# Value products of an attention as half-row pairs of two heads, with the other TensorE work gathered in fewer places

## The reference

```python
xn, ln = layernorm(ctx), layernorm(latents)          # 77 and 1024 rows of 256
q = (ln @ Wq) -> 16 heads of 64;  k, v = concat([xn, ln]) @ Wkv -> 16 heads of 64
qn, kn = rmsnorm(q) * 64**-0.5, rmsnorm(k)
attn = softmax(where(mask, qn @ kn.T, -max))         # 1024 queries x 1101 keys
x = x + (attn @ v) @ Wout + bout
x = x + moe(layernorm(x))                            # shared expert + top 2 of 8, gelu
```

## Time and profile before

| what | us |
|---|---|
| median of 3 runs | 2591.28 (2587.12 to 2591.97) |
| the profiled execution | 2582.26 |
| its span, first to last instruction | 2580.4 |
| TensorE busy (matmuls) | 2469.2, 96% |
| TensorE weight loads | 1899.8, 74% |
| VectorE, ScalarE, GpSimdE busy | 1737.1, 1677.3, 1275.5 |
| TensorE's mean granted clock | 0.984 of 2.4 GHz |

### The profile page before, as it was taken

One profiled execution on the slowest core, in us unless ns is written; L12 is line 12 of the kernel. 1 busy time (PEld: TensorE's weight loads), 2 busy tenths in 40 slices (PEclk: granted clock), 3 DMA queues, 4 the chain that ended last, 5 costly groups with the idle time before them and its releaser, 6 DMA issues. The chain is left out here.

```text
span 2580.4 us, 46535 instructions
## 1 busy us (share of the span) xinstructions
PE 2469.2 (96%) x15720; PEld 1899.8 (74%) x15720; DVE 1737.1 (67%) x2516; ACT 1677.3 (65%) x2286; POOL 1275.5 (49%) x783
## 2 busy tenths in 40 slices
PE   3799999999999999999999999997989999999997
PEld 3566666666666666666666666656989999999997
DVE  7666766666667666676666666765876557767675
ACT  2577877787778777787788777883333344454443
POOL 4445434453455445543455344522534526666665
PEclk8899999999999999999999999998989999999999
DMA  5423422233223322332223322246822459999996
GB/s 182 155 81 92 129 87 76 84 121 104 82 78 125 103 78 86 99 121 86 78 88 122 97 82 78 86 124 128 175 84 77 141 185 318 326 317 319 323 323 170
DMA packets 231441, 361.76 MB, mean 140 GB/s; under 512 B 59559, under 2 KB 139739, under 8 KB 227400
## 3 DMA queue, kind: packets, MB, share of 16 engines
q1 hardware_dynamic: 204694, 301.66, 38.0%
q0 software_dynamic: 25696, 58.82, 8.2%
q10 hardware_dynamic: 978, 0.34, 0.1%
HBM read 280.90 MB, written 79.85 MB: 140 GB/s over the span
## 5 line engine op out<-in xcount | busy, mean ns | idle before, releaser
L826 ACT ACTIVATE pr_hi<-ps_s 128x1024 fp32r<-128x1024 f32 x512 | 524.6, 1025 | 262.0 <-PE ps_s L948 260.7
L717 DVE TENSOR_TENSOR pr_lo<-ps_s,pr_hi 128x1024 fp32r<-128x1024 f32 x288 | 351.8, 1221 | 257.1 <-ACT ps_s L827 256.9
L962 PE MATMUL ps_o<-pr_hi,vA 128*65 128x512 f32 x1152 | 472.4, 410 | 1.4 <-DVE o_first L646 0.8
L717 DVE TENSOR_TENSOR pr_lo<-pr,pr_hi 128x1024 fp32r<-128x1024 f32 x288 | 354.3, 1230 | 163.7 <-ACT pr L827 163.7
L964 PE MATMUL ps_o<-pr_lo,vA 128*65 128x512 f32 x1152 | 454.0, 394 | 0.0
L963 PE MATMUL ps_o<-pr_hi,vC 128*65 128x512 f32 x1152 | 452.9, 393 | 0.0
L455 POOL TENSOR_TENSOR sq<-raw 128x1024 f32<-128x1024 f32 (+1 forms) x96 | 134.1, 1397 | 625.3 <-ACT raw L771 625.3
L1613 ACT ACTIVATE ht<-f_ps_h,b 128x256 f32<-128x256 f32 x440 | 184.5, 471 | 339.6 <-PE f_ps_h L1545 306.4
L1545 PE MATMUL f_ps_h<-xT_hi,w 128*128 128x256 f32 x1760 | 355.1, 285 | 2.4 <-DVE xT_lo L1647 2.3
L917 PE MATMUL ps_m<-w_sb,lnT_sb 128*128 128x384 f32 (+1 forms) x1728 | 349.2, 341 | 4.2 <-DVE q_lo L659 2.5
L917 PEld LDWEIGHTS ps_m<-w_sb,lnT_sb 128*128 128x128 f32 x1728 | 298.2, 191 | 59.7 <-issue 36.4
(11 more groups left out here) (214 smaller groups left out, 4394.9 us busy)
## 6 DMA issues: line engine op xcount, KB each, us to landing
w<-w1S_dram SPq DMA_DIRECT2D x160, 512.0 KB, 6.3
lnT_sb<-lnT_dram SPq DMA_DIRECT2D x31, 2304.0 KB, 9.0
w2raw<-in_L_ffn_Wproj SPq DMA_DIRECT2D x78, 512.0 KB, 6.4
w1S_dram<-cut POOLq DMA_DIRECT2D x36, 512.0 KB, 3.0
rec<-rden_dram SPq DMA_DIRECT2D x63, 256.0 KB, 3.7
routed_dram<-empty POOLq DMA_DIRECT2D x28, 387.0 KB, 3.6
xt<-routed_dram SPq DMA_DIRECT2D x39, 258.0 KB
w_raw<-in_L_xattn_Wkv SPq DMA_DIRECT2D x66, 128.0 KB, 3.7
```

The lines of the kernel that those rows point to most:

```text
L717: v.tensor_tensor(pr_lo[:, ring(w, d), :], full_of(d), pr_hi[:, ring(w, d), :].bitcast(F32), ALU.subtract).then_inc(s_lo, 1)
L826: act.activation(pr_hi[:, ring(w, d), :], ps_s[:, d % 2, :], ACT.Exp, bias=bias)
L962: mm(out, upper, pr_hi[:, r, cols], start=k == 0, stop=False)
```

## The change

- Value products become products of 64 rows (`values_half`). A key tile's upper 64 keys and its lower 64 keys are given to the two heads at the same time, one head in rows 0 to 63 and the other in rows 64 to 127, each into its own bank; a unit later (part 1) the same tile is done with the two halves swapped. In each step of the loop the second half of unit d - 3 and the first half of unit d - 2 have the same assignment of rows to banks. A unit has six pairs, three in each part. The second part waits for its own first part (`s_half`). Only the very last units keep 128-row products.
- TensorE goes unit by unit: scores, jobs, second half, first half; at units 2 and 11 (`BETWEEN`), where a group ends, the jobs stand between the halves.
- Jobs are gathered: turns two by two at units 2 and 4 and one at 6, projections at 6 (one) and two by two at 8, 11, 13, 15. They stay 128-row products; `project_halves` is there for units in `HALVED`, which is empty.
- The full exponentials go to `pr` in units 0, 1, 9, 16 and 17 (`SPARED`), else back to `ps_s`; the waits follow.
- VectorE copies both heads' outputs in one instruction, once both are done; `invert`, `divide`, `squares` and `values` move to other units.

```diff
+TURNED = {2: (0, 1), 4: (2, 3), 6: (4,)}
+PROJECTED = {6: (0,), 8: (1, 2), 11: (3, 4), 13: (5, 6), 15: (7, 8)}
+HALVED = ()
+BETWEEN = (2, 11)
+SPARED = (0, 1, 9, 16, 17)
...
-            return pr[:, 0, :] if d % 2 else ps_s[:, 0, :]
+            return pr[:, d % 2, :] if d in SPARED else ps_s[:, d % 2, :]
...
-                wait(dve, s_pv0, w.n(2, h + 1 - 2 * before))
-                v.tensor_copy(o_sb[h][0:DH + 1, 0:512], ps_o[0:DH + 1, 0, :]).then_inc(s_o, 1)
                 wait(dve, s_pv, w.n(UNITS, KT * (h + 1) - UNITS * before))
-                v.tensor_copy(o_sb[h][0:DH + 1, 512:N], ps_o[0:DH + 1, 1, :]).then_inc(s_o, 1)
+                v.tensor_copy(o_sb[h][0:DH + 1, :].rearrange("p (r n) -> p r n", r=2), ps_o[0:DH + 1, :, :]).then_inc(s_o, 1)
...
-                            if d == 3:
+                            if d == 5:
                                 invert(w, 1, 1)
-                            if d == 7:
+                            if d == 9:
                                 divide(w, 1, 1)
-                        if w.attend and d == 12:
+                        if w.attend and d == 13:
                             invert(w, 0, 0)
...
-                        if w.turn and d in (2, 4):
-                            values(w, d == 4)
-                        if w.proj and d in (11, 15):
-                            squares(w, (d - 11) // 4)
+                        if w.turn:
+                            for i in TURNED.get(d, ()):
+                                turned(w, i)
+                        if w.turn and d in (3, 5):
+                            values(w, d == 5)
+                        if w.proj and d in (14, 17):
+                            squares(w, (d - 14) // 3)
...
-                        if d == 0 and not (isinstance(w.v, int) and (w.v == -1 or 2 * w.v + w.s == WINDOWS - 1)):
+                        if d == 2 and not (isinstance(w.v, int) and (w.v == -1 or 2 * w.v + w.s == WINDOWS - 1)):
                             squares(w, 2 - GROUPS)
...
-                        if d % 2:
+                        if d in SPARED:
                             wait(act, s_lo, w.n(UNITS, d - 1))
...
+            def weights(w, d):
...
+                return g, k, [(v_[:, slot, k, :, 0:DH + 1], p_[:, r, :]) for v_, p_ in ((vA, pr_hi), (vC, pr_hi), (vA, pr_lo))]
+
+            def begin(w, d, g, k):
+
+                pe.wait_ge(s_lo, w.n(UNITS, d + 1))
+                if k == 0:
+                    wait(pe, s_o, w.n(2, g))
...
+            def values_half(w, d, part, swap):
+
+                g, k, pairs = weights(w, d)
+                if part == 0:
+                    begin(w, d, g, k)
+                else:
+                    pe.wait_ge(s_half, w.n(UNITS, d + 1))
+                for i, (v_, p_) in enumerate(pairs):
+                    for t in range(2):
+                        h, rows = t ^ swap, slice(DH * t, DH * t + DH)
+                        ins = mm(ps_o[0:DH + 1, h, :], v_[rows, h], p_[rows, 512 * h:512 * h + 512],
+                                 start=k == 0 and part == 0 and i == 0, stop=k == KT - 1 and part == 1 and i == 2)
+                ins.then_inc(s_pv if part else s_half, 1)
...
+                    def second(d):
+                        if w.attend and not (w.first and d < LAG + 1):
+                            values_half(w, d - LAG - 1, 1, d % 2)
+
+                    def first(d):
                         if w.attend and not (w.first and d < LAG):
                             if d == LAG:
                                 pe.wait_ge(s_v, w.n(2, 2))
-                            values(w, d - LAG)
-
-                    for d in range(0, UNITS, 2):
+                            if last and d == UNITS - 1:
+                                values(w, d - LAG)
+                            else:
+                                values_half(w, d - LAG, 0, d % 2)
+
+                    for d in range(UNITS):
...
-                            wait(pe, s_lo, w.n(UNITS, d - 1))
+                            wait(pe, s_exp if (d - 2) % UNITS in SPARED else s_lo, w.n(UNITS, d - 1))
                             scores(w, d, general)
-                            if general and (d + 1) % KT == 0:
-                                maximum(w, (d + 1) // KT)
-                            wait(pe, s_exp, w.n(UNITS, d))
-                            scores(w, d + 1, general)
...
+                        elif d in BETWEEN:
+                            second(d)
+                            jobs(d)
+                            first(d)
                         else:
-                            job(d)
-                            weigh(d)
-                            job(d + 1)
-                            weigh(d + 1)
+                            jobs(d)
+                            second(d)
+                            first(d)
```

More of the change, by code:

```diff
@@ L77 @@
 TURNS = len(PARTS)
-FIRST_TURN = 2
-FIRST_PROJ = FIRST_TURN + TURNS
+TURNED = {2: (0, 1), 4: (2, 3), 6: (4,)}
[3 more added lines that the diff above has]
+SPARED = (0, 1, 9, 16, 17)
 JOBS = TURNS + KT
@@ L300, in spread @@
                 half = w.n(2, g - 2 * before)
-                wait_then(s_o, w.n(4, 2 * g + 2 - 4 * before))
+                wait_then(s_o, w.n(2, g + 1 - 2 * before))
                 sp.dma_start(rden[bass.ds(half, 1)].unsqueeze(0), o_sb[g][DH:DH + 1, :].unsqueeze(1)).then_inc(s_put, 16)
@@ L829, in window @@
                         upper(d)
[L830 to L833, removed]
+                    if w.turn:
+                        for i in TURNED.get(d, ()):
+                            turned(w, i)
+                    if w.proj:
+                        for tile in PROJECTED.get(d, ()):
+                            projected(w, tile)
                     if isinstance(w.v, int) and w.v == -1:
@@ L900, in turn, with ready @@
                 ins.then_inc(s_job, 1)
-            def project(w, tile):
-                out = ps_m[:, tile % 2, :]
+            def ready(w, tile):
                 if tile < 2:
@@ L914, in project @@
                     pe.wait_ge(s_wlo, w.n(1, 3))
-                lo = 0 if tile < NT else PW
-                for k, (a, b, c) in enumerate((a, b, c) for a, b in ((0, 0), (0, 1), (1, 0)) for c in range(C)):
+            products = [(a, b, c) for a, b in ((0, 0), (0, 1), (1, 0)) for c in range(C)]
+            def project(w, tile):
+                ready(w, tile)
+                out, lo = ps_m[:, tile % 2, :], 0 if tile < NT else PW
+                for k, (a, b, c) in enumerate(products):
                     ins = mm(out[:, lo:3 * PW], lnT_sb[:, a, c, tile * P:(tile + 1) * P], w_sb[:, w.slot, b, c, lo:],
@@ L919, in project, with project_halves @@
                 ins.then_inc(s_job, 1)
+            def project_halves(w, n, tiles, part):
+                for k, (a, b, c) in enumerate(products):
+                    for j, tile in enumerate(tiles):
+                        if part == 0 and k == 0:
+                            ready(w, tile)
+                        if part == 1 and k == 0 and j == 0:
+                            pe.wait_ge(s_jobhalf, w.n(len(HALVED), 2 * len(HALVED) + n + 1))
+                        rows = slice(DH * (j ^ part), DH * (j ^ part) + DH)
+                        lo, last = 0 if tile < NT else PW, part == 1 and k == 3 * C - 1
+                        ins = mm(ps_m[:, tile % 2, lo:3 * PW], lnT_sb[rows, a, c, tile * P:(tile + 1) * P],
+                                 w_sb[rows, w.slot, b, c, lo:], start=part == 0 and k == 0, stop=last)
+                        if last:
+                            ins.then_inc(s_job, 1)
+                if part == 0:
+                    ins.then_inc(s_jobhalf, 1)
             def maximum(w, g):
@@ new lines, in values @@
+            def values(w, d):
+                g, k, pairs = weights(w, d)
+                begin(w, d, g, k)
+                for h in range(2):
+                    for i, (v_, p_) in enumerate(pairs):
+                        ins = mm(ps_o[0:DH + 1, h, :], v_[:, h], p_[:, 512 * h:512 * h + 512],
+                                 start=k == 0 and i == 0, stop=k == KT - 1 and i == 2)
+                ins.then_inc(s_pv, 1)
+            def values_half(w, d, part, swap):
+                g, k, pairs = weights(w, d)
+                if part == 0:
+                    begin(w, d, g, k)
+                else:
+                    pe.wait_ge(s_half, w.n(UNITS, d + 1))
+                for i, (v_, p_) in enumerate(pairs):
+                    for t in range(2):
[3 more added lines that the diff above has]
+                ins.then_inc(s_pv if part else s_half, 1)
@@ L969, in pe_windows @@
             def pe_windows(general):
                 def window(w):
-                    def job(d):
-                        if w.turn and FIRST_TURN <= d < FIRST_TURN + TURNS:
-                            turn(w, d - FIRST_TURN)
-                        if w.proj and FIRST_PROJ <= d < FIRST_PROJ + KT:
```

(16 more changed lines are left out.)

26 lines of the change are left out of this document (8 added, 18 removed).

## The result

The changed kernel takes 2639.48 us (median of 4 runs, 2636.55 to 2643.64), the kernel before took 2590.93 in the same comparison (2587.12 to 2591.97): a ratio of 1.0194, interval 1.0179 to 1.0209. It is slower by 48.5 us, where 12.5 us faster was forecast.

What follows compares the result with a forecast made beforehand. TensorE's stream was taken as the bound. Gains less stalls gave 0.55 us a window, 16.5 over 30 windows, less 6 at the start, plus 2 at the end: 12.5 us faster, 2579 us, range 2550 to 2606.

Steps and rivals of the forecast that it cites:

- Half-row pairs: Value products: six 128-row products of a unit become six 64-row pairs at equal cost; 0, bounds +-0.2 us a window.
- round trips: TensorE's switches between 64-row and 128-row work: seven a window, not nine; 0.70 us gained, bounds 0 and 0.9.
- turns and invert: Per window: turns gathered in twos gain 0.2 us; `invert` two units later removes VectorE's transfer wait and gains 0.40.
- weight loads of pairs would stand in the open: Rival: each value pair's weight load waits for the pair ahead, adding 473 us, about 3060 us; chance 0.02.
- The undivided copy: At unit 2, TensorE waits for VectorE's copy of both heads' outputs: 0.55 us lost a window, bounds 0 and 1.4.
- VectorE and GpSimdE at the window's seam: Squares moved to later units make GpSimdE's chain and VectorE's copy tight: 0.2 us lost a window, bounds 0 and 0.5.
- GpSimdE's chain sets the seam: Rival: long normalisation of group 0 holds squares 1 and VectorE, and TensorE stalls; 26 us slower, 2617; chance 0.20.
- Ahead of the first window: Before attention starts, squares 0 and 1 come later with nothing to hide them: +6.1 us together, bounds 2 and 8.

Runs made afterwards that it cites:

- whole_values: Changed kernel with the value products as 128-row products of one head, in the new order and still in TensorE's loop: 2702.57 us, ratio 1.0458 to the kernel before.
- unrolled_squares_13: Changed kernel with TensorE's windows written out and group 0's squares after unit 13 instead of 14: 2548.83 us, ratio 0.9864 to the kernel before.
- copy_covered: unrolled_squares_13 with the second half put ahead of the unit's scores at units 2 and 11: 2550.38 us, ratio 0.9868 to the kernel before.
- squares_13: Changed kernel, TensorE's loop kept, with group 0's squares after unit 13 instead of 14: 2609.36 us, ratio 1.0089 to the kernel before.
- unrolled: Changed kernel with TensorE's loop over the windows written out one after another: 2605.85 us, ratio 1.0084 to the kernel before.

## Why the prediction was wrong, point by point

- *Half-row pairs, 0; round trips, 0.70; turns and invert, 0.60.* Right. Pairs run at 0.23, whole_values prices the round trip at 0.39 where 0.35 was taken, no turn waits for q_lo any more (11.3 us in the earlier trace rows), and `invert` (L678) idles 0.0 us where it waited 1.26. With the two stalls out of the way (unrolled_squares_13) the window is 51.23; these terms and the copy's give 52.40 - 1.30 + 0.55 = 51.65, so together they were 0.4 us too cautious; which of them, no run shows.
- *The rule that weight loads of pairs would stand in the open.* Wrong here, as the prediction said: 0.23 us a pair leaves no room for 0.134 us of load.
- *The undivided copy, 0.55.* Right: 0.45 to 0.46 us idle at unit 2, released by the copy, and 0.53 us came back where copy_covered removed it.
- *"VectorE and GpSimdE at the window's seam", 0.2, bounds 0 and 0.5.* This step failed. It measured 1.57 us. The step added up GpSimdE's chain and VectorE's instructions by their means from a trace in which nrm alone paid for lying beside VectorE: 1.21 for the division, 1.22 for a lower half, 1.89 for sq. In their new places they took 2.90, 2.31 and 2.87. The rival that GpSimdE's chain sets the seam named the place and the waits, but looked for nrm to run long and for `squares` to wait; instead nrm ran short and VectorE's own instructions were the late ones. The sign was among the rows: nrm took 3096 ns for the 1024 elements for which sq took 1890.
- *The loop's code.* This cost was put at nothing, and it is the larger of the two: in no term and in no rival. The change was counted as products exchanged one for one in time, never as instructions: 790 products with loads a turn, not 574. Its price, from squares_13 and unrolled_squares_13, is (2609.36 - 2548.83) / 13 = 4.7 us a turn.
- *Ahead of the first window, +6 (2 to 8).* 1.9 us, a little under the lower bound.
- *The sum.* 51.23 + 13 x 4.48 / 30 (with the one turn that was measured above) + 17 x 1.57 / 30 (seams that no turn hides) = 54.06 of the 54.34 us measured.

The Trainium skill, Runtime: NRT & Kernel Launch, section "Instruction fetch mechanics", says that code comes in blocks of 16 KiB fetched in order, and that a taken branch to code that is not held stops the engine until it has come. The trace agrees with the blocks (16.4 KB a packet) and with the stop: the branch takes 3.35 to 3.95 us where packets come at the turn, and 0.21 to 0.24 where none do. It also says that fetching in order is hidden because instructions are issued more slowly than code comes in: the trace of unrolled agrees, with 126 packets and no idle time of TensorE that no other engine ends.

## What to carry to other kernels

Where one instruction becomes two that run side by side, count instructions too: the length of each engine's loop body, the packets of the instruction queue in the steady part of the trace, and how long the loop's branch takes against the products in hand. Where steps of two engines are moved onto each other, don't price them by means from a trace in which they lay otherwise; look for the same operation at two durations there. And when an early store or load is made earlier still, ask what queues behind it.

## What the runs showed of the hardware that was not expected

- One division, same shape and line: 1209 ns alone, 2905 beside GpSimdE's sq, which itself stretches from 1.89 to 2.87 us.
- The same code loads cost nothing where the windows are written out (126 packets), nothing at a turn of the new order with 128-row products (111 packets), 0.6 to 0.7 us at three of six turns of the old order, and about 4.7 us at a turn of the 64-row stream. The branch waits 3.4 to 3.7 us in the median in all three; 14 products handed over ahead of it last 1.5 us as 64-row pairs, 16 or 17 last 3.3 to 3.5 as 128-row ones. With a load of 2304 KB beside it the branch took 4.29.
- After an idle time of 2.33 us TensorE ran at half pace (0.43 us a pair, the lower of its two clock levels) from about 1073.6 to 1076.2, at a granted clock of 0.50 there (0.79 over the 8 us).
- The kernel before, written out, got slower by 0.15 to 0.34%: with instruction packets on the queues its waits for q_lo grew from 11.3 to 19.8 us, behind a later `den` transfer (37.8 to 46.7). Why that transfer is later stays open.
